# Routed experts in one fused kernel: tiles sorted by the chunk of their first row, and pick rows summed beside the last expert groups

## The chip, the cores and the metric

The kernel runs on one core of a Trainium2 chip. The metric is the device time of one execution in microseconds. Three runs of the kernel before took 598.46, 595.2 and 590.54 us, median 595.2. The profile is of one execution; its times count from the first instruction.

## The reference, cut to what matters

Everything is in 32-bit floats. A token is a row of 256 numbers; there are 4096.

```python
x = layernorm(x + attention(x))                       # 4096 tokens x 256, 16 heads
scores = sigmoid(x @ router_weight.T)                 # 32 experts in 4 groups of 8
topk_idx = the 4 best of the experts in the 2 best groups (by scores + bias)
topk_w   = 2.5 * scores[topk_idx] / sum of them
for each token and each of its 4 picks e:
    h = silu(x @ gate_w[e].T) * (x @ up_w[e].T)       # 128 wide
    mixed += topk_w * (h @ down_w[e].T)               # back to 256
shared = (silu(x @ sg.T) * (x @ su.T)) @ sd.T         # 256 wide, every token
x = layernorm(x + mixed + shared)
```

## The kernel before

**Chunks.** The tokens are cut into 8 chunks of 512 (four tiles of 128). Attention, first layernorm, router and shared expert run chunk by chunk, software-pipelined in an order written out by hand for each engine. In `route` and `place` VectorE finds each token's four experts and its rank within each expert; ranks are counted over all chunks so far by `count_picks` on TensorE, whose result ScalarE copies to `ranks_sb` (its last 32 columns are the running totals per expert, which start at 128). POOL then scatters each token's row, with its label and weight, to the expert's region in DRAM (`scatter_rows`, 128 indirect DMAs, L534). The rows of an expert therefore lie in the order of the tokens.

**The table.** When all chunks are ranked, VectorE works out which tiles of 128 rows there are (from L1677, 14 steps that wait for each other by the semaphore `b`): for each expert as many tiles as it needs, aligned to the end of its rows, the experts one after the other. TensorE transposes the result, VectorE packs it into `tab`, and the engines read tile addresses and expert numbers from it.

**The expert loop.** The tiles are worked off in groups of four, a group being two pairs. There are 34 groups in this run (136 tiles). In each pair SP loads two tiles of rows (L477), TensorE turns them over (L1292) and multiplies by gate and up weights, ScalarE copies the transposed rows (L876) and takes the tanh (L894), VectorE copies the next pair's gate and up weights from the big weight tile to a fixed place (`copy_weights`, L1754), forms the gated product (L1779, L1785) and copies labels (L1747, L1762, L1769), TensorE multiplies by the down weights one pair later, ScalarE scales and copies the result (`copy_y`, L885), and POOL scatters the result rows by label to `pick_rows` in DRAM (L568), where the four rows of a token lie together. Each engine has its own loop over the groups, written once in `quads_with_ends` with the first and the last group apart; they meet only through semaphores. Two buffers stand behind each step.

**The tail.** When the last scatter has landed, SP reads all `pick_rows` back, chunk by chunk in the order 5, 6, 7, 0, 1, 2, 3, 4 (`LAST_ORDER`), four loads of 512 KB each into four buffers (L494). VectorE adds picks 0 and 1 to 2 and 3 (`add_picks`, L1804), TensorE sums the two halves and the token's own row `sx` in PSUM through an identity matrix (`sum_rows`, L1348, L1350), with the shared expert's down product for the chunks 5 to 7 (`sum_down`). For chunks 0 to 4 `sx` holds that product already. VectorE takes mean and variance (`moments`), POOL the reciprocal root (`invert_sums`, L583), ScalarE scales (`finish`, L912) and issues the write of the output (L918). `matmul` is recorded at L933 wherever the helper `mm` issues it.

Of the kernel before, what the change touches and what calls it, by code (L numbers as in the profile page):

```python
# [13 lines left out]
P = 128  # L14
# [10 lines left out]
EPS = 1e-5  # L25
# [9 lines left out]
ZWAYS = 4  # L35
# [7 lines left out]
LAST_ORDER = (5, 6, 7, 0, 1, 2, 3, 4)  # L43
# [14 lines left out]
assert MAXTILES + QUAD <= SLOTS  # L58

# [5 lines left out]
def build(nc, xT, x, wqkv, wfc, wr, rbias, wsgu, wsd, wgu, wd, out):  # L65
# [7 lines left out]
    with ExitStack() as ctx:  # L73
# [76 lines left out]
        def x1_of(b):  # L150
# [25 lines left out]
        dstats = [sb(f"dstats{i}", [P, TPC, 6]) for i in range(2)]  # L176
        dmv = [sb(f"dmv{i}", [P, TPC, 2]) for i in range(2)]
        dveps = [sb(f"dveps{i}", [P, TPC]) for i in range(2)]
        drstd = [sb(f"drstd{i}", [P, TPC]) for i in range(2)]
        dnm = [sb(f"dnm{i}", [P, TPC]) for i in range(2)]  # L180

        cnt_u = sb("cnt_u", [P, NE], U32)
        ntile_u = sb("ntile_u", [P, NE], U32)
        ntile = sb("ntile", [P, NE])
        tend = sb("tend", [P, NE])
        ones_e = over(prod, 25 * DM - NE, NE)
        past = sb("past", [P, 2, NE])
        pend = sb("pend", [P, 2, NE])
        slot_e = sb("slot_e", [P, 2])
        slot_first = sb("slot_first", [P, 2])  # L190
        slot_base = sb("slot_base", [P, 2])
        spare = sb("spare", [P, NE + 1])
        jump = sb("jump", [P, NE])
# [21 lines left out]
        zt = [over(wgu_sb, i * TPC * TOPK * DM, TPC * TOPK, DM).rearrange("p (t k) c -> p t k c", k=TOPK)  # L215
              for i in range(ZWAYS)]
        o2 = [over(wd_sb, i * TPC * DM, TPC, DM) for i in range(2)]
# [13 lines left out]
        d_a d_ps dst_ready dmv_ready dveps_ready drstd_ready dnm_ready o2_ready stored0 stored1""".split()  # L231
# [6 lines left out]
        z_loaded = [[sem(f"z_loaded{i}_{t}") for t in range(TPC)] for i in range(ZWAYS)]  # L238
        stored = [S[f"stored{i}"] for i in range(2)]

        NSMALL = 5 * 16
        NCONST = 12
# [3 lines left out]
        block = ctx.enter_context(nc.Block())  # L246

# [5 lines left out]
        def n_quads(eng):  # L253
            eng.wait_ge(S["tab_ready"], 1)
            return eng.value_load(tab[0:1, QUADS:QUADS + 1], min_val=NTOK * TOPK // P // QUAD - 2,
                                  max_val=(MAXTILES + QUAD - 1) // QUAD - 2) + 2
# [11 lines left out]
        def _(sp):  # L268
# [216 lines left out]

            for par in range(2):
                sp.wait_ge(y_scattered[par], quads * 32)

            for g in range(CH):
                if g >= ZWAYS:  # L490
                    sp.wait_ge(S["d_ps"], TPC * (g - ZWAYS + 1))
                for t in range(TPC):
                    at = (LAST_ORDER[g] * TPC + t) * P
                    sp.dma_start(zt[g % ZWAYS][:, t, :, :],  # L494
                                 z.rearrange("(n k) c -> n k c", k=TOPK)[at:at + P, :, :])\
                        .then_inc(z_loaded[g % ZWAYS][t], 16)

        @block.gpsimd
        def _(pool):
# [24 lines left out]
            assert NCONST == 12  # L524
# [54 lines left out]
            def invert_sums(g, step, first, last):  # L579
                pool.wait_ge(S["dveps_ready"], step + 1)  # L580
                if g >= 2:
                    pool.wait_ge(S["o2_ready"], g - 1)
                pool.tensor_tensor(drstd[g % 2][:, first:last], dveps[g % 2][:, first:last], neg_half[:, first:last],  # L583
# [7 lines left out]
        def quads_with_ends(eng, quads, body):  # L591
            body(0, 0, False, True)
            body(0, 1, True, True)
            with eng.Fori(1, quads - 1) as quad:
                body(quad, 0, True, True)
                body(quad, 1, True, True)
            body(quads - 1, 0, True, True)
            body(quads - 1, 1, True, False)

        @block.scalar  # L600
        def _(act):
# [298 lines left out]

            copy_xT(0, 0)
            quads_with_ends(act, quads, pairs)
# [995 lines left out]
```

## Time and profile before

| | |
|---|---|
| runs of the kernel | 598.46, 595.2, 590.54 us, median 595.2 |
| profiled execution | span 591.0 us (its time outside the span isn't recorded) |
| PE (TensorE) | busy 557.3 us, 94% |
| DVE (VectorE) | busy 372.0 us, 63% |
| ACT (ScalarE) | busy 278.8 us, 47% |
| POOL | busy 289.8 us, 49% |
| moved by DMA | 135.34 MB, 229 GB/s over the span |
| expert loop | about 311 to 526 us |
| reads of the tail | 32 loads of 512 KB, 14.7 us from issue to landing in the median |

A busy share is time in which an engine had an instruction under way. Matmuls are pipelined, and one that waits for its predecessor counts as busy, so a TensorE at 100% isn't at its peak. "issue" as the cause of idle time means that nothing the profile shows held the engine up. A releaser is the work whose end let the waiting instruction start.

### The profile page before, as it was taken

Reading aid. Unit: us, or ns where it says so; the run is one execution under the profiler, and the core shown is the slowest. Engines: PE = TensorE matmul, PEld = TensorE weight load, DVE = VectorE, ACT = ScalarE, POOL = GpSimd, SP = SyncE. Lnnn points to the kernel's source line nnn. Section 1 sums busy time; section 2 is a strip of 40 time slices with the busy share of each in tenths; the row PEclk is TensorE's granted clock in tenths of the full one; section 3 lists DMA queues with packets and bytes.
Section 4 is the critical chain, followed back from the end, with each engine's and each line's share of the span. In section 5 each row is a group of like instructions: output and inputs, shape, how many; then the busy total and the mean of one; then the engine's idle time right before and its main releaser. Section 6 shows DMA issues by size and latency. Waiting matters only on the chain.

```text
span 591.0 us, 16304 instructions
## 1 busy us (share of the span) xinstructions
PE 557.3 (94%) x4916; PEld 437.1 (74%) x4917; DVE 372.0 (63%) x1250; ACT 278.8 (47%) x561; POOL 289.8 (49%) x301
## 2 busy tenths in 40 slices
PE   5989999999989999999969999999999999999985
PEld 2446578677665766675529999999999999887863
DVE  2032657698885887679544666666666665634774
ACT  2334453765837575253213555555555554530234
POOL 5000000654777765667741666666666665660221
PEclk9999999999999999999987999999999999999998
DMA  7999978987899799799423555555555554528996
GB/s 260 249 237 230 236 220 201 277 271 193 267 248 287 224 322 391 268 395 343 171 93 96 168 165 164 162 172 163 160 167 168 180 171 153 172 91 353 414 413 246
DMA packets 125820, 135.34 MB, mean 229 GB/s; under 512 B 76872, under 2 KB 107087, under 8 KB 125136
## 3 DMA queue, kind: packets, MB, share of 16 engines
q1 hardware_dynamic: 108288, 95.92, 54.3%
q0 software_dynamic: 12672, 34.10, 15.2%
q10 hardware_dynamic: 4816, 4.74, 2.3%
q8 instruction: 27, 0.44, 0.3%
q14 instruction: 17, 0.14, 0.1%
HBM read 74.79 MB, written 60.96 MB: 230 GB/s over the span
## 4 chain that ended last, share of the span: by engine, by line
PE 63%; DMA 15%; SPq 6%; issue 5%; POOL 4%; DVE 3%; ACT 2%; ACTq 0%; POOLq 0%; DVEq 0%
PE bank L933 54%; PE bank L1292 5%; DMA wgu_sb<-pick_rows 4%; DMA o_slots<-wgu_sb 4%; DMA wd_sb<-o_slots 3%; POOL expert_rows L534 3%; PE bank L1350 2%; DMA expert_rows<-stage,pos 2%; SPq L319 1%; SPq L328 1%; SPq L299 1%; PE bank L1348 1%; PE bank L981 1%; DMA q_slots<-wd_sb 1%; SPq L285 1%
## 5 line engine op out<-in xcount | busy, mean ns | idle before, releaser
L568 POOL DMA_INDIRECT pick_rows<-prod,ids x134 | 131.2, 979 | 93.9 <-ACT prod L885 46.2
L534 POOL DMA_INDIRECT expert_rows<-stage,pos x128 | 129.1, 1008 | 57.0 <-issue 34.8
L933 PE MATMUL bank<-prod 128*128 128x128 f32 x1088 | 135.0, 278 | 1.0 <-issue 1.0
L933 PEld LDWEIGHTS bank<-prod 128*128 128x128 f32 x1088 | 128.9, 195 | 1.7 <-issue 1.6
L933 PE MATMUL bank<-wd_sb,wqkv_sb 128*128 128x512 f32 x192 | 91.5, 614 | 6.5 <-DMA wqkv_sb<-in_wqkv 5.9
L1754 DVE COPY prod<-wgu_sb 128x512 f32 x136 | 54.1, 440 | 54.5 <-issue 51.8
L885 ACT ACTIVATE prod<-bank,kept 128x256 f32<-128x256 f32 x136 | 57.0, 470 | 37.7 <-PE bank L933 35.1
L933 PEld LDWEIGHTS bank<-wgu_sb 128*32 128x32 f32 x2048 | 58.6, 136 | 16.8 <-issue 13.6
L933 PE MATMUL bank<-wd_sb,prod 128*128 x272 | 70.1, 380 | 0.8 <-DVE prod L1785 0.8
L933 PE MATMUL bank<-wgu_sb 128*32 128x64 f32 x2048 | 65.8, 296 | 2.2 <-DMA wgu_sb<-k_slots 2.2
L933 PEld LDWEIGHTS bank<-wd_sb,wqkv_sb 128*128 128x128 f32 x192 | 35.1, 194 | 41.6 <-issue 35.8
L527 POOL TENSOR_TENSOR rstdt<-vepst,neg_half 128x4 f32<-128x4 f32 x8 | 9.0, 1129 | 100.2 <-DVE vepst L1396 100.2
L894 ACT ACTIVATE prod<-bank 128x256 f32<-128x256 f32 x68 | 26.1, 384 | 61.2 <-PE bank L933 61.2
L933 PEld LDWEIGHTS bank<-wd_sb,prod 128*128 128x128 f32 x272 | 46.5, 191 | 4.7 <-issue 1.2
L933 PE MATMUL bank<-prod,wsgu_sb 128*128 128x512 f32 x96 | 45.1, 618 | 2.8 <-DVE hsT L1461 2.8
L1292 PE MATMUL bank<-ident,prod 128*128 128x128 f32 x272 | 41.9, 278 | 3.1 <-DMA prod<-expert_rows 3.1
L876 ACT ACTIVATE prod<-bank 128x512 f32<-128x512 f32 x68 | 40.6, 597 | 4.2 <-PE bank L1292 4.2
L1292 PEld LDWEIGHTS bank<-ident,prod 128*128 128x128 f32 x272 | 34.4, 143 | 10.8 <-DMA prod<-expert_rows 4.2
L1414 DVE TENSOR_REDUCE smax<-bank 128x32 f32<-128x512 f32 x16 | 10.9, 679 | 47.2 <-PE bank L933 47.2
L618 ACT ACTIVATE stage<-sx 128x1024 f32<-128x1024 f32 x32 | 34.1, 1067 | 9.7 <-DMA expert_rows<-stage,pos 7.1
L912 ACT ACTIVATE wd_sb<-bank,dnm,drstd 128x256 f32<-128x256 f32 x32 | 15.6, 563 | 45.4 <-DVE dnm L1811 25.9
L933 PEld LDWEIGHTS bank<-prod,wsgu_sb 128*128 128x128 f32 x96 | 18.2, 196 | 24.0 <-issue 19.7
(148 smaller groups left out, 774.6 us busy)
## 6 DMA issues: line engine op xcount, KB each, us to landing
prod<-expert_rows SPq DMA_DIRECT2D x136, 132.0 KB
wgu_sb<-pick_rows SPq DMA_DIRECT2D x32, 512.0 KB, 14.7
wgu_sb<-in_wgu SPq DMA_DIRECT2D x2, 2560.0 KB, 13.4
expert_rows<-pad_rows SPq DMA_DIRECT2D x4, 1056.0 KB, 19.0
wd_sb<-in_xT SPq DMA_DIRECT2D x8, 512.0 KB, 4.8
q_slots<-wd_sb SPq DMA_DIRECT2D x16, 256.0 KB
k_slots<-wd_sb SPq DMA_DIRECT2D x16, 256.0 KB
wgu_sb<-q_slots SPq DMA_DIRECT2D x16, 256.0 KB
```

What stands on the lines that cost most here:

```text
L534: pool.indirect_dma_start(xs, bass.IndirectOffsetOnAxis(ap=pos[e % 2][:, i, k:k + 1], axis=0), stage[:, i, k, :], None, bounds_check=XROWS ...
L568: pool.indirect_dma_start(z, bass.IndirectOffsetOnAxis(ap=index[:, j:j + 1], axis=0), rows[:, j, :], None, bounds_check=TOPK * NTOK - 1, o ...
L618: act.activation(stage[:, i, :, 0:DM], x1_of(e)[:, i, :].unsqueeze(1).broadcast_to([P, TOPK, DM]), ACT.Copy)
L876: act.activation(xtT[par][:, :], banks[2][:, :], ACT.Copy).then_inc(S["cX_copied"], 1)
L885: last = act.activation(to[:, j, :], banks[6 + par][:, j * DM:(j + 1) * DM], ACT.Copy, scale=kept[par][:, j, 1:2])
L894: act.activation(cth[par][:, :], banks[par][:, 0:2 * P], ACT.Tanh, scale=0.5)\
L912: done = act.activation(o2[g % 2][:, t, :], banks[2 * (g % 4) + t // 2][:, (t % 2) * DM:(t % 2 + 1) * DM], ACT.Identity, bias=dnm[g % 2][: ...
L933: return pe.matmul(dst, lhsT, rhs, start=(k == 0), stop=(k == n - 1))
L1292: last = pe.transpose(banks[2][:, c:c + P], xt[par][:, j, k * P:(k + 1) * P], ident[:, :])
L1350: last = pe.matmul(sum_of(g, t), ident[:, :], zt[g % ZWAYS][:, t, k, :], start=False, stop=(k == 1 and (b < DOWN_AT_ONCE or t % 2 == 1)))
L1414: dve.tensor_reduce(smax[:, hf, :], score_view(hf), AX, ALU.max).then_inc(S["smax"], 1)
L1754: last = dve.tensor_copy(ws[par][:, j, :], wgu_sb[:, bass.ds(expert(word, slot + j) * (KC * 2 * EI), KC * 2 * EI)])
```

## The change

Tiles are no longer listed expert by expert. Each belongs to one of six classes: the chunk (0 to 4, or later) in which its first row lies. The table lists class by class, and by expert within a class. To this end `place` keeps the running totals of the first five chunks (`cums`), and the table is worked out for 6 x 32 = 192 virtual experts. The number of tiles is the same. After the early classes are through, all picks of the early chunks have been computed, some groups before the end; assertions bound by how much.

That is used twice. In each of the 16 groups ahead of the last, ScalarE loads one tile of 128 tokens of the chunks 0 to 3 (their 4 x 256 pick values, 512 KB) after the group's first pair, and VectorE adds them to `sx` in three additions after its second pair. And SP loads chunk 4 when four groups are left. The tail then reads the chunks 5, 6 and 7 only. The chunks 0 to 3 take their statistics directly from `sx`; outputs are written in place in `sx` and stored from there, in the order 0 to 7, and the waits on output buffers are gone.

```diff
+def groups_behind(c):
+    left = NTOK * TOPK - (c + 1) * CT * TOPK
+    return -(-(left - NE * (P - 1)) // P) // QUAD
+SUM_LAG = 3
+SUM_GROUPS = FIRST_TILES            # 16
+SUM_START = SUM_GROUPS + 1
+LATE_GROUPS = groups_behind(FIRST_CHUNKS)      # 4
...
+        early_z = wsgu_sb.rearrange("p k c -> p (k c)")
+        early_sum = wqkv_sb.rearrange("p k c -> p (k c)")[:, 2 * CT:2 * CT + 2 * DM]
...
 # SP
+            for par in range(2):
+                sp.wait_ge(y_scattered[par], quads * 32 - 32 * LATE_GROUPS)
+            load_picks(FIRST_CHUNKS)
             for par in range(2):
                 sp.wait_ge(y_scattered[par], quads * 32)
-            for g in range(CH):
-                if g >= ZWAYS:
-                    sp.wait_ge(S["d_ps"], TPC * (g - ZWAYS + 1))
...
+            for g in range(FIRST_CHUNKS + 1, CH):
+                load_picks(g)
...
-        def quads_with_ends(eng, quads, body):
+        def quads_with_ends(eng, quads, body, beside=None):
             body(0, 0, False, True)
             body(0, 1, True, True)
-            with eng.Fori(1, quads - 1) as quad:
+            with eng.Fori(1, quads - (SUM_START if beside else 1)) as quad:
                 body(quad, 0, True, True)
                 body(quad, 1, True, True)
+            if beside:
+                with eng.Fori(0, SUM_GROUPS) as tile:
+                    quad = eng.snap(eng.to_reg(quads - SUM_START + tile))
+                    body(quad, 0, True, True)
+                    beside(quad, tile, 0)
+                    body(quad, 1, True, True)
+                    beside(quad, tile, 1)
 # ScalarE
+            def load_early(quad, tile, par):
+                if par:
+                    return
+                act.wait_ge(S["e_free"], tile + 1)
+                for i in range(2):
+                    act.wait_ge(y_scattered[i], quad * 32 - 32 * SUM_LAG)
+                act.dma_start(early_z[:, :], z.rearrange("(n k) c -> n (k c)", k=TOPK)[bass.ds(tile * P, P), :])\
+                    .then_inc(S["e_z"], 16)
 # VectorE
             def place(e):
                 dve.wait_ge(S["rk"], RK * e + 1)
+                if e < CLASSES - 1:
+                    dve.tensor_copy(cums[:, e, :], ranks_sb[:, TPC, :])
...
+            at(dve.tensor_tensor(classes(behind_u[:, NE:], CLASSES - 1),
+                                 total.unsqueeze(1).broadcast_to([P, CLASSES - 1, NE]), cums[:, :, :], ALU.subtract))
...
+            at(dve.tensor_tensor(lens[:, :], whole[:, 0:VE], whole[:, NE:], ALU.subtract))
...
+            at(dve.tensor_tensor_scan(tend[:, :], ones_v[:, :], lens[:, :], 0.0, ALU.mult, ALU.add))
...
+            def sum_early(quad, tile, par):
+                if par == 0:
+                    return
+                dve.wait_ge(S["e_z"], tile * 16 + 16)
+                dve.tensor_tensor(early_sum[:, :], early_z[:, 0:2 * DM], early_z[:, 2 * DM:], ALU.add)\
+                    .then_inc(S["e_free"], 1)
+                dve.wait_ge(S["e_free"], tile + 2)
+                dve.tensor_tensor(early_sum[:, 0:DM], early_sum[:, 0:DM], early_sum[:, DM:], ALU.add)\
+                    .then_inc(S["e_half"], 1)
+                dve.wait_ge(S["e_half"], tile + 1)
+                dve.tensor_tensor(sx[:, bass.ds(tile * DM, DM)], sx[:, bass.ds(tile * DM, DM)], early_sum[:, 0:DM],
+                                  ALU.add).then_inc(S["e_sum"], 1)
...
+            dve.wait_ge(S["e_sum"], FIRST_TILES)
+            moments(0, 0, TPC)
+            moments(1, 0, TPC)
+            add_picks(4, range(TPC))
+            moments(2, 0, TPC)
+            scale_mean(0, 0, 0, TPC)
...
-BSTEPS = 14
+BSTEPS = 22
```

## Rows read from the trace of the kernel before

**Rows 1.** Windows by stage: window, length, busy us of each engine, clock, DMA share, GB/s

```profile
0.00:309.00 309.00, 289.44 (x3044) 189.94 (x3045) 197.16 (x660) 146.86 (x257) 145.51 (x156) 0.99 0.85 257
...
365.00:502.00 137.00, 137.00 (x1064) 130.06 (x1062) 88.95 (x308) 75.39 (x177) 85.50 (x89) 1.00 0.53 167
...
536.00:580.50 44.50, 41.01 (x185) 33.83 (x183) 32.22 (x95) 9.76 (x21) 8.30 (x6) 1.00 1.03 410
```

**Rows 2.** Timeline of VectorE, one group: start, length, line, operation, [idle before <-releaser]

```profile
441.88 0.77 DVE L1754 COPY prod<-wgu_sb 128x512 f32 x2 [0.79 <-issue]
...
443.39 0.16 DVE L1762 CAST ids<-kept 128x2 uint32<-128x2 f32 x1
443.69 0.35 DVE L1769 COPY kept<-meta 128x4 f32<-128x4 f32 x1
...
448.06 0.76 DVE L1754 COPY prod<-wgu_sb 128x512 f32 x2 [0.79 <-issue]
```

**Rows 3.** Timeline of all engines in the same group, ScalarE's part

```profile
442.18 0.38 ACT L894 ACTIVATE prod<-bank 128x256 f32<-128x256 f32 x1 [0.82 <-PE bank L933]
...
443.05 0.84 ACT L885 ACTIVATE prod<-bank,kept 128x256 f32<-128x256 f32 x2 [0.48 <-PE bank L933]
```

**Rows 4.** Timeline of all engines around a late scatter, 500 to 515 us

```profile
500.11 0.17 DVE L1762 CAST ids<-kept 128x2 uint32<-128x2 f32 x1 [1.03 <-DMA pick_rows<-prod,ids]
...
503.11 2.02 PE L933 MATMUL bank<-prod 128*128 128x128 f32 x16 [0.96 <-issue]
...
508.37 0.92 DVE L1754 COPY prod<-wgu_sb 128x512 f32 x2 [0.82 <-PE bank L933]
...
514.64 0.90 DVE L1754 COPY prod<-wgu_sb 128x512 f32 x2 [0.83 <-PE bank L933]
```

**Rows 5.** VectorE by line and form: busy us, mean ns of one, idle before, releaser

```profile
L1785 DVE TENSOR_TENSOR prod<-prod,bank 128x256 f32<-128x256 f32 x68 | 28.7, 421 | 5.3
...
L1804 DVE TENSOR_TENSOR wgu_sb<-wgu_sb 128x512 f32<-128x512 f32 x32 | 21.7, 690 | 22.1 <-DMA wgu_sb<-pick_rows 22.0
```

**Rows 6.** DMA issues: count, KB each, median us from issue to landing

```profile
wd_sb<-in_xT SPq DMA_DIRECT2D x8, 512.0 KB, 4.8
...
prod<-in_x SPq DMA_DIRECT2D x8, 512.0 KB, 5.6
```

**Rows 7.** Timeline of all engines in the tail

```profile
530.15 0.97 POOL L568 DMA_INDIRECT pick_rows<-prod,ids_last  x1 [0.30 <-issue]
532.61 17.64 SPq L494 DMA_DIRECT2D wgu_sb<-pick_rows  x23
...
535.90 0.69 DVE L1804 TENSOR_TENSOR wgu_sb<-wgu_sb 128x512 f32<-128x512 f32 x1 [10.02 <-DMA wgu_sb<-pick_rows]
...
553.72 1.93 ACT L912 ACTIVATE wd_sb<-bank,dnm,drstd 128x256 f32<-128x256 f32 x4 [3.06 <-DVE dnm L1811]
...
555.68 0.38 ACTq L918 DMA_DIRECT2D out<-wd_sb  x1
...
580.90 1.29 DVE L1804 TENSOR_TENSOR wgu_sb<-wgu_sb 128x512 f32<-128x512 f32 x2
```

**Rows 8.** Timeline where the table is worked out, VectorE and TensorE

```profile
281.71 0.17 DVE L1677 TENSOR_SCALAR cnt_u<-ranks_sb 128x32 uint32<-128x32 f32 x1
...
284.22 0.16 DVE L1702 TENSOR_TENSOR slot_row<-slot_base,slot_first 128x2 f32<-128x2 f32 x1
...
285.01 0.69 DVE L1461 SCALAR_TENSOR_TENSOR hsT<-hsT,bank 128x512 f32<-128x512 f32 x1
...
287.55 7.03 PE L933 MATMUL bank<-prod,wsgu_sb 128*128 128x512 f32 x16
```

**Rows 9.** Windows where TensorE stood idle, and one behind

```profile
32.90:35.10 2.20, 0.04 (x1) 0.00 (x0) 0.00 (x0) 0.60 (x1) 0.00 (x0) 1.00 1.07 281
...
296.00:298.50 2.50, 0.31 (x2) 0.00 (x1) 2.05 (x4) 1.08 (x2) 1.94 (x2) 1.00 0.30 108
...
301.00:303.50 2.50, 2.50 (x4) 0.94 (x4) 0.00 (x0) 0.00 (x0) 1.94 (x2) 0.54 0.30 108
```

More of the change, by code:

```diff
@@ L42 @@
 DOWN_AT_ONCE = 5
[L43 removed]
+SUM_BANKS = {4: 6, 5: 0, 6: 2, 7: 4}
 ROW = DM + 8
@@ L58 @@
 assert MAXTILES + QUAD <= SLOTS
+def groups_behind(c):
[4 more added lines that the diff above has]
+SUM_START = SUM_GROUPS + 1
+for _t in range(FIRST_TILES):
+    assert SUM_START - _t + SUM_LAG <= groups_behind(_t // TPC)
+LATE_GROUPS = groups_behind(FIRST_CHUNKS)
+COUNTED_FROM = SUM_START + SUM_LAG + 2
+assert LATE_GROUPS == 4 and NTOK * TOPK // P // QUAD > COUNTED_FROM
 def chunk(n):
@@ L175, in build @@
         pos = [sb(f"pos{i}", [P, TPC, TOPK], U32) for i in range(2)]
[L176 to L188, printed above, removed]
+        late = wsel.rearrange("p t k e -> p (t k e)")
+        dstats = [over(late, g * TPC * 6, TPC, 6) for g in range(CH)]
+        dmv = [over(late, 192 + g * TPC * 2, TPC, 2) for g in range(CH)]
+        dveps = [over(late, 256 + g * TPC, TPC) for g in range(CH)]
+        drstd = [over(late, 288 + g * TPC, TPC) for g in range(CH)]
+        dnm = [over(late, 320 + g * TPC, TPC) for g in range(CH)]
+        cums = sb("cums", [P, CLASSES - 1, NE])
+        region_e = sb("region_e", [P, NE])
+        behind_u = over(prod, 0, VE).bitcast(U32)
+        whole_u = over(prod, VE, VE).bitcast(U32)
+        whole = over(prod, 2 * VE, VE + NE)
+        ends = over(prod, 3 * VE + NE, NE)
+        first_row = over(prod, 3 * VE + 2 * NE, VE + NE)
+        lens = over(prod, 4 * VE + 3 * NE, VE)
+        tend = over(prod, 5 * VE + 3 * NE, VE)
+        past = over(prod, 6 * VE + 3 * NE, 2, VE)
+        pend = over(prod, 8 * VE + 3 * NE, 2, VE)
+        assert 10 * VE + 3 * NE <= 2048
+        jump = over(wfc_sb.rearrange("p k c -> p (k c)"), 0, VE)
+        ones_v = over(wfc_sb.rearrange("p k c -> p (k c)"), VE, VE)
         slot_e = sb("slot_e", [P, 2])
+        slot_u = sb("slot_u", [P, 2], U32)
+        slot_m = sb("slot_m", [P, 2], U32)
         slot_first = sb("slot_first", [P, 2])
         slot_base = sb("slot_base", [P, 2])
-        spare = sb("spare", [P, NE + 1])
-        jump = sb("jump", [P, NE])
         slot_row = sb("slot_row", [P, 4])
@@ L213, in build @@
         ws = [over(prod, 8 * DM + 4 * ROW + 8 * P + i * 2 * KC * 2 * EI, 2, KC * 2 * EI) for i in range(2)]
[L215 to L217 removed]
+        early_z = wsgu_sb.rearrange("p k c -> p (k c)")
+        early_sum = wqkv_sb.rearrange("p k c -> p (k c)")[:, 2 * CT:2 * CT + 2 * DM]
+        zt = {g: over(wgu_sb, (g - 5) * TPC * TOPK * DM, TPC * TOPK, DM).rearrange("p (t k) c -> p t k c", k=TOPK)
+              for g in range(FIRST_CHUNKS + 1, CH)}
+        zt[FIRST_CHUNKS] = over(stage.rearrange("p t k r -> p (t k r)"), 0, TPC * TOPK, DM)\
+            .rearrange("p (t k) c -> p t k c", k=TOPK)
         banks = [bank(f"bank{i}") for i in range(8)]
@@ L1687, in _ @@
+            after()
             for c in range(2):
@@ new lines, in _ @@
+            scale_mean(3, 3, 0, TPC)
+            moments(4, 0, TPC)
+            add_picks(5, (2, 3))
+            scale_mean(4, 4, 0, TPC)
+            add_picks(6, (0, 1))
+            moments(5, 0, TPC)
+            add_picks(6, (2, 3))
+            add_picks(7, (0, 1))
+            scale_mean(5, 5, 0, TPC)
+            moments(6, 0, TPC)
+            add_picks(7, (2, 3))
+            moments(7, 0, 2)
+            scale_mean(6, 6, 0, TPC)
+            moments(7, 2, TPC)
+            scale_mean(7, 7, 0, 2)
```

183 lines of the change are left out of this document (92 added, 91 removed).

## The prediction

> **What bounds the kernel now.** I read the windows by stage first, then the chain of waits, then the loop engine by engine. In the stages [rows 1] the reader is to see two limits. From 365 to 502 us, the steady part of the expert loop, TensorE is busy in all 137 us at full clock while VectorE shows only 89 us of work and the DMA engines half a share. From 536 to 580.5 us the DMA share is 1.03 at 410 GB/s: this is the tail that reads all pick rows back (16.8 MB) while it writes outputs. The chain of waits names reads of pick rows for most of it. So the tail is paid in bytes, the loop in TensorE time, and the change moves bytes from the tail into the loop.
>
> The 65% of VectorE in the loop misleads. A group (two pairs, four tiles) repeats every 6.18 us: the weight copy at 441.88 comes again at 448.06 [rows 2]. Before each weight copy stands 0.8 us of "issue", which is sequencer work (the value load and its address arithmetic) that no other engine holds up. The tanh that the next step needs [rows 3] ends at 442.56, before VectorE's own weight copies do (442.65): it waits for nobody there.
>
> The trace holds an accident that tests this [rows 4]. At 500.11 VectorE had waited 1.03 us for a scatter; TensorE then stood idle 0.96 us before 503.11. Nearly all of it passed through. Nor was it made good: from 508.37 to 514.64 a group took 6.27 us. **VectorE's own chain is as long as TensorE's.** Whatever is put into it lengthens the loop.
>
> **The change, part by part.**
>
> *Early sums, 16 groups.* After the second pair of each group VectorE waits for an early load and does three dependent additions, one of 128x512 and two of 128x256. Prices: 0.69 us for 128x512 (the pick addition of the tail) and 0.42 for 128x256 (the second gate product) [rows 5], 1.53 in all. With hops of 0.03 between dependent steps and some 0.15 of register work before the first wait, the chain from the label cast to the next kept copy becomes 0.15 + 0.72 + 0.45 + 0.05 + 0.34 = 1.71 us in place of the 0.30 between 443.39 and 443.69 [rows 2]; that 0.30 is the loop's branch, now hidden under the last addition. Added: 1.4, and I take 1.5 for the register arithmetic on the tile number. The group then takes 6.25 + 1.5 = 7.75 us against 6.18: 1.57 x 16 = **+25 us**. Lower bound: 1.2 per group (the additions' 1.53 less the 0.30 hidden), +19. Upper: 2.2 (all three start to start, with 0.6 of register work), +35. TensorE, ScalarE and POOL then wait; none of them adds to it.
>
> *The early load.* ScalarE issues it after it has copied the y rows of the previous pair. That copy needs the kept labels, which VectorE now makes only after its additions. Counted from their end: 0.4 for the kept copy, 0.84 for the two y copies [rows 3], 0.38 for the issue (as in rows 7), so about 1.6 to 1.8. VectorE needs the rows at 7.75 - 1.5 = 6.25. The load may take 4.5 us. Loads of the same 512 KB took 4.8 and 5.6 us from issue to landing [rows 6], in a stage whose DMA share is 0.85 [rows 1]; the loop has 0.53, and with the load (0.52 MB at 410 GB/s is 1.28 us of 7.75) about 0.6. The first load of the tail, with the engines free, is issued at 532.61 and its addition starts at 535.90 [rows 7], 3.3 us. Between 3.3 and 5.6 I take 4.6, a share of 0.6 lying between the two: **+1.5 us** over 16 groups for what comes late. Its end points are 0 and 16 x (1.8 + 5.6 - 6.25) = 18. On ScalarE the issue stands ahead of the next xT copy, which has over 1 us in hand.
>
> The Trainium skill ("DMA: Bandwidth & Descriptors", section "Anatomy of one DMA — SWDGE (gpsimd) path") gives about 2.0 us plus bytes at 436 GB/s for the software path; taken as an estimate here that would be 3.2 us for 512 KB, and the load would never be late. The rows show longer landings, in busier stretches.
>
> *Other work in the loop.* Counters for groups gain a few register steps on each engine; a third loop body costs a fresh start of code. Chunk 4's four loads go out on SP's queue, past the last row loads, which are issued by then, and meet the last scatters: **+1 us** together, between 0 and 3.
>
> *The tail.* The reads fall from 32 to 12 loads of 512 KB, 16.8 to 6.3 MB. SP still waits for the last scatter, whose landing sets the start at 532.6. VectorE meanwhile does the statistics of chunks 0 and 1 and adds chunk 4, but the reciprocal roots of POOL stand behind its scatters until 531.1, so the first output write goes out near 537, and then one of 512 KB each 2.3 us (1.93 for four activations, 0.38 for the issue). Until the last read lands the engines move 6.3 MB of reads and about 3.1 of writes: 9.4 MB / 410 GB/s = 23 us, plus 1.5 of ramp: near 557. In the profile the last pair of pick additions starts at 580.90 and the span ends 10.1 later; that closing chain is unchanged. 580.9 - 557 = **-23.5 us**. Bounds: no write before the last read, -29; all 4.2 MB of writes first, -20. VectorE's work for eight chunks of statistics and four of additions is some 27 us, spread from 526 on, so it isn't the limit but near it.
>
> *The table.* Tiles get 192 virtual experts where there were 32. The chain from 281.71 to 284.38 [rows 8] has 14 steps; now 22, most 192 to 384 wide. From 0.16 us for 2 elements [rows 8] and 0.69 for 512 [rows 5] an element costs 1.04 ns: some 2,430 more elements give 2.5 us, eight steps at 0.12 another 1.0: 3.5 us longer. Behind it stands the gate product (285.01) that the gate matmuls at 287.55 wait for; they start 1.7 us later, and of that some 1.5 us reaches the loop's start, through the last gate product, which stands ahead of the first weight copy on VectorE. Five more copies of 32 columns in the placement, 0.2 each, lie partly beside POOL: **+2 us** in all, between 0 and 4.5. The number of tiles stays the same, since the same whole tiles are only sorted otherwise.
>
> **The sum.** 25 + 1.5 + 1 + 2 - 23.5 = +6; I keep **+5**, as the tail's start may gain a little from less crowded last groups. The span 591.0 becomes 596. No time of the profiled execution is given beside its span; the span stands 4.2 under the median of 595.2, which I carry over: **600 us**.
>
> **Rivals.**
> 1. *The additions fall into VectorE's idle time* (faster). For it: 0.8 us of "issue" before each weight copy, two per group, looks like room for 1.5 us. Against: the sequencer itself is at work there, and rows 4 show a delay going through. If only 0.4 per group remains: 6.4 + 1 + 2 - 23.5 = -14, 581 us. It decides once the loop grows by less than 0.5 us a group. The low bounds of all terms (19 + 0 + 0 + 0 - 29) end at -10. Chance 0.15.
> 2. *The load lands late* (slower). ScalarE's issue waits for the kept labels, these for the additions, these for the load: a ring, where each microsecond of landing beyond 4.5 is paid 16 times. At 5.6 us it costs 18 in place of 1.5: +21, 616 us; at 5.2, 610. It decides from 5.0 us. With the additions at their upper bound the same sign comes out. Chance 0.25.
> 3. *TensorE's clock falls.* Its idle stretch would be 1.6 us in each group. At 296 to 298.5 us TensorE was idle 2.2 us, and the granted clock then fell to its lower level, 1.2 GHz (0.54 as a mean of 301 to 303.5); after another 2.2 us at 32.9 it stayed at 2.4 GHz [rows 9]. Part of a group at the lower level costs about 1.2 us (2.5 x 0.46), most of which the idle stretch absorbs. Only with late loads would idle stretches pass 2 us; +10 on top, 610 to 625. Chance 0.04, part of slower. The Trainium skill ("TensorE: Matmul & The Clock Gate", section "What's actually happening") says that the slow state is the default and activity releases it; by that the thinner loop is at risk. The trace has both outcomes for the same idle time.
>
> The forecast keeps 0.56. **How the numbers follow.** A change of 2% is 11.9 us, about what a measurement of this kernel can tell from no change: faster is under 583.3, slower over 607.1. Faster gets 0.16 (rival 1 and a corner of the bounds), slower 0.27 (rivals 2 and 3 with the upper bound of the additions), within 0.57. The range reaches from 586 (additions and tail near their better bounds) to 616 (rival 2 at 5.6 us), leaving a tenth outside on each side.
>
> **What would show it.** Timeline of VectorE in the last groups: weight copy to weight copy every 7.6 to 7.9 us over two pairs, the 128x512 addition waiting for the DMA under 0.3 us, TensorE idle 1.6 us before one of two gate stages. Groups before them at 6.18. Last pick addition about 24 us after the start of the tail's reads, not 48. A loop start 1 to 3 us later. I am wrong if early groups stay near 6.2 us (rival 1), or if the additions name the DMA for over a microsecond each (rival 2).

## The result, and the profile after

The changed kernel takes **604.2 us** (median of 6 runs, 601.85 to 605.41) against 596.9 us (590.54 to 599.53) for the kernel before beside it: ratio **1.0149**, 95% interval 1.0110 to 1.0187. Slower by 1.5%. The profiled run took 601.85 us around a span of 600.1 us, 9.1 us more than the 591.0 of before. Here and below the ratios are over fast runs alone and the medians over all runs, so the two don't agree to the last digit.

Windows by stage of the changed kernel (length, busy us of PE, PEld, DVE, ACT, POOL, then clock, DMA share, GB/s). They answer to [rows 1]; the loop now has two stages, in the first two rows; the third is the tail.

```profile
330.00:420.00 90.00, 90.00 (x702) 85.53 (x700) 58.62 (x204) 49.74 (x117) 56.81 (x59) 1.00 0.53 163
443.00:553.00 110.00, 86.81 (x632) 76.31 (x631) 68.61 (x224) 47.21 (x106) 50.98 (x53) 1.00 0.60 191
569.50:589.50 20.00, 20.00 (x94) 17.61 (x93) 13.02 (x45) 10.82 (x23) 4.90 (x5) 1.00 0.98 376
```

Up to 420 us the loop is the old one. From 443 to 553 us, in the early groups, TensorE works in 79% of the time. The tail's window is 20 us where it was 44.5, and the DMA engines are full in it as before.

VectorE's timeline through one early group, which answers to [rows 2] (start, length, line, operation, idle before):

```profile
463.68 0.76 DVE L1820 COPY prod<-wgu_sb 128x512 f32 x2 [1.14 <-issue]
...
465.57 0.17 DVE L1813 COPY meta<-prod 128x4 f32<-128x4 f32 x1
466.81 0.80 DVE L1820 COPY prod<-wgu_sb 128x512 f32 x2 [1.07 <-PE bank L983]
...
468.31 0.33 DVE L1828 CAST ids<-kept 128x2 uint32<-128x2 f32 x1
468.38 0.69 DVE L1862 TENSOR_TENSOR wqkv_sb<-wsgu_sb 128x512 f32<-128x512 f32 x1
469.10 0.42 DVE L1865 TENSOR_TENSOR wqkv_sb<-wqkv_sb 128x256 f32<-128x256 f32 x1
469.69 0.42 DVE L1868 TENSOR_TENSOR sx<-sx,wqkv_sb 128x256 f32 x1 [0.16 <-DVE wqkv_sb L1865]
470.50 0.17 DVE L1835 COPY kept<-meta 128x4 f32<-128x4 f32 x1 [0.38 <-issue]
470.77 0.17 DVE L1813 COPY meta<-prod 128x4 f32<-128x4 f32 x1
472.11 0.76 DVE L1820 COPY prod<-wgu_sb 128x512 f32 x2 [1.17 <-issue]
```

A "meta copy" here is the copy of a pair's labels and weights out of the loaded rows, a "kept copy" the second copy of them, by which the results are scaled and scattered, a "cast" the one that makes row numbers of the labels. Three readings. The group takes 472.11 - 463.68 = **8.43 us** against 6.18. The first addition starts 0.07 us after the label cast: it waits for no read. From cast to kept copy it is 2.19 us in place of 0.30, and from each meta copy to its weight copy 1.24 and 1.34 us, where the plain loop has about 1.0, as in this half of a group before:

```profile
444.14 0.17 DVE L1747 COPY meta<-prod 128x4 f32<-128x4 f32 x1
445.13 0.82 DVE L1754 COPY prod<-wgu_sb 128x512 f32 x2 [0.82 <-issue]
```

TensorE in the same group, and at the first early groups, where the granted clock fell once (a gate stage of 16 matmuls took 3.55 us and not 2.02):

```profile
429.80 3.55 PE L983 MATMUL bank<-prod 128*128 128x128 f32 x16 [2.79 <-ACT prod L919]
...
464.55 2.02 PE L983 MATMUL bank<-prod 128*128 128x128 f32 x16 [1.70 <-ACT prod L919]
```

The tail, answering to [rows 7] (the second row is the last pair of pick additions):

```profile
569.10 6.19 SPq L523 DMA_DIRECT2D wgu_sb<-pick_rows  x12
...
590.02 1.40 DVE L1884 TENSOR_TENSOR wgu_sb<-wgu_sb 128x512 f32<-128x512 f32 x2
```

From the start of the reads to that pair it is 20.9 us, against 580.90 - 532.61 = 48.3.

**The account.** Cut both spans at the start of the loop's third gate stage (318.01 us after, 319.71 before) and at the end of the last down matmul (561.83, 526.54). Ahead of the loop -1.7, loop +37.0, tail 38.3 against 64.5 = -26.2: together +9.1. The tail gave what was asked of it, and the loop cost more than that. The -1.7 is noise: the first gate stage happened to run at the lower clock before (3.62 us) and at full clock after (2.02), and in the 14 profiles of this case the second group's first weight copy starts anywhere from 316.4 to 323.2 us, over code that hardly differs up to there.

### The profile page after: what moved, and what is told of

The parts are those of the page before. It is cut to its first block, busy times and chain, and to the rows that moved or that the text cites. A ratio compares the mean times of both kernels' runs of the same rounds, so it can differ in the third digit from the quotient of the medians.

```text
span 600.1 us, 16345 instructions
## 1 busy us (share of the span) xinstructions
PE 543.7 (91%) x4820; PEld 419.1 (70%) x4821; DVE 383.9 (64%) x1294; ACT 281.9 (47%) x561; POOL 287.1 (48%) x302
## 4 chain that ended last, share of the span: by engine, by line
PE 59%; DMA 11%; DVE 10%; issue 7%; DVEq 4%; ACT 3%; SPq 3%; POOL 2%; ACTq 1%; POOLq 0%
PE bank L983 54%; PE bank L1342 3%; DMA wgu_sb<-pick_rows 2%; DVEq L293 2%; DMA prod<-expert_rows 2%; DMA expert_rows<-stage,pos 2%; DVE prod L1820 1%; DVE prod L1845 1%; PE bank L1031 1%; DMA pick_rows<-prod,ids 1%; DVE wqkv_sb L1862 1%; DVE wqkv_sb L1865 1%; DVE ids L1828 1%; DMA o_slots<-wgu_sb 1%; DMA wd_sb<-o_slots 1%
## 5 line engine op out<-in xcount | busy, mean ns | idle before, releaser
L572 POOL DMA_INDIRECT expert_rows<-stage,pos x128 | 127.8, 999 | 59.2 <-issue 33.8
L983 PE MATMUL bank<-wd_sb,wqkv_sb 128*128 128x512 f32 x192 | 92.8, 621 | 6.7 <-DMA wqkv_sb<-in_wqkv 6.0
L983 PE MATMUL bank<-wd_sb,prod 128*128 x272 | 70.1, 380 | 1.2 <-DVE prod L1851 1.2
L1342 PEld LDWEIGHTS bank<-ident,prod 128*128 128x128 f32 x272 | 32.6, 141 | 17.1 <-issue 9.5
L983 PEld LDWEIGHTS bank<-prod,wsgu_sb 128*128 128x128 f32 x96 | 18.2, 196 | 23.9 <-issue 19.7
L670 ACT ACTIVATE wd_sb<-bank 128x512 f32<-128x512 f32 x32 | 19.4, 608 | 27.8 <-PE bank L983 25.3
```

The costliest lines, as they stand in the source:

```text
L572: pool.indirect_dma_start(xs, bass.IndirectOffsetOnAxis(ap=pos[e % 2][:, i, k:k + 1], axis=0), stage[:, i, k, :], None, bounds_check=XROWS ...
L670: act.activation((QT, KT)[j // 2][:, j % 2, :], banks[j % 2][:, :], ACT.Copy)\
L983: return pe.matmul(dst, lhsT, rhs, start=(k == 0), stop=(k == n - 1))
L1342: last = pe.transpose(banks[2][:, c:c + P], xt[par][:, j, k * P:(k + 1) * P], ident[:, :])
```

## The experiments

All ratios are to the kernel before, in the runs beside them. The means are over the 15 whole groups, weight copy to weight copy, that hold early additions; "loop" is from the second group's first weight copy to the last weight copy of all, "rest" from there to the end of the span.

| Kernel | median us | ratio (95%) | group, mean us | loop | rest |
|---|---|---|---|---|---|
| before | 596.9 | 1 | 6.30 | 202.9 | 70.1 |
| after | 604.2 | 1.0149 (1.0110 to 1.0187) | 8.58 | 239.3 | 44.4 |
| additions one column wide | 596.4 | 1.0011 (0.9971 to 1.0052) | 7.89 | 228.0 | 44.7 |
| no early reads | 602.7 | 1.0130 (1.0069 to 1.0191) | 8.41 | 236.6 | 44.5 |
| early groups written out | 602.2 | 1.0167 (1.0088 to 1.0246) | 8.23 | 233.3 | 44.2 |
| before, sorted table | 596.5 | 1.0012 (0.9972 to 1.0051) | | | |
| second loop, no additions | 605.5 | 1.0123 (1.0064 to 1.0183) | 6.84 | 211.6 | 70.6 |
| additions on GpSimd | 667.2 | 1.1215 (1.1156 to 1.1275) | 11.92 | 293.4 | 49.8 |
| chunk 4 read in the tail | 616.1 | 1.0322 (1.0271 to 1.0372) | 8.57 | 239.0 | 52.8 |
| chunk 0 read one a group | 595.6 | 0.9997 (0.9962 to 1.0032) | 6.58 | 206.7 | 66.8 |
| chunk 0 read at the end | 596.1 | 0.9976 (0.9927 to 1.0024) | 6.30 | 206.9 | 67.9 |
| base outside the loop | 600.3 | 1.0072 (1.0031 to 1.0113) | 8.26 | 235.8 | 44.4 |
| base outside, written out | 599.1 | 1.0074 (1.0035 to 1.0113) | 8.13 | 233.9 | 45.0 |
| the same, no early reads | 585.3 | 0.9830 (0.9781 to 0.9879) | 7.22 | 217.9 | 46.8 |

For each the same 15 groups are meant, also where they hold no additions. The profiled run of the sorted table took 601.3 us, 4.8 above that kernel's median, so its loop isn't compared. The kernels with narrow additions or without early reads leave out part of the result, the sums of chunks 0 to 3.

### What the additions' width costs

```
-    dve.tensor_tensor(early_sum[:, :], early_z[:, 0:2 * DM], early_z[:, 2 * DM:], ALU.add)
+    dve.tensor_tensor(early_sum[:, 0:1], early_z[:, 0:1], early_z[:, 2 * DM:2 * DM + 1], ALU.add)
```

The two additions behind it are cut to one column in the same way, so the sums of chunks 0 to 3 are left out.

> The three additions of each early group keep their place, their waits and their registers, but are one column wide instead of 512, 256 and 256, so the sums of chunks 0 to 3 are left out. Theory A (VectorE's own chain sets the group): the widths are worth about 0.5 + 0.25 + 0.25 = 1.0 us of the 8.42 us of a group, so a group takes 7.4 us, and the time falls by 16 us against the changed kernel, to about 588. The 1.2 us that then still lie above 6.18 are waits between dependent steps and register work. Theory B (the early load, through ScalarE's queue, sets the group): a group stays at 8.2 to 8.4, time 601 to 604.

Measured: 596.4 us, no different from the kernel before, and groups of 7.72 us at best. VectorE's timeline in that kernel:

```profile
498.89 0.32 DVE L1828 CAST ids<-kept 128x2 uint32<-128x2 f32 x1
498.96 0.25 DVE L1862 TENSOR_TENSOR wqkv_sb<-wsgu_sb 128x1 f32<-128x1 f32 x1
499.27 0.16 DVE L1865 TENSOR_TENSOR wqkv_sb<-wqkv_sb 128x1 f32<-128x1 f32 x1
499.59 0.16 DVE L1868 TENSOR_TENSOR sx<-sx,wqkv_sb 128x1 f32 x1 [0.16 <-DVE wqkv_sb L1865]
500.39 0.17 DVE L1835 COPY kept<-meta 128x4 f32<-128x4 f32 x1 [0.64 <-issue]
```

With next to no elements, cast to kept copy still takes 1.50 us. The elements are 0.69 us of the 2.24 added a group; the other 1.55 are there without them, and the runs below take them apart. I had put 1.0 us to the elements and 1.2 to the rest, and so expected 588. Theory B falls: a group doesn't stay at 8.2 to 8.4.

### Whether the read is what VectorE waits for

```
-    act.dma_start(early_z[:, :], z.rearrange("(n k) c -> n (k c)", k=TOPK)[bass.ds(tile * P, P), :])...
-    dve.wait_ge(S["e_z"], tile * 16 + 16)
```

The additions then add what lies in the buffer; the sums of chunks 0 to 3 are left out.

> The 16 early loads and VectorE's wait for them are left out; the three additions run over what lies there, so the sums of chunks 0 to 3 are left out. Theory A: VectorE waits only some 0.1 us for the load, so a group stays within 0.2 us of 8.42 and the time falls by 1 to 4 us (the first groups, where the load was late, and the DMA queues), to 600 to 603. Theory B: a group falls to 7.7 us or less and the time by 11 us or more, to 593 or less.

Measured: 602.7 us, steady groups of 8.37 to 8.45, such as this one (8.40 us):

```profile
476.42 0.76 DVE L1818 COPY prod<-wgu_sb 128x512 f32 x2 [1.18 <-issue]
...
484.82 0.76 DVE L1818 COPY prod<-wgu_sb 128x512 f32 x2 [1.15 <-issue]
```

**Rival 2 falls**: without reads the steady group is as long. Only the first two early groups differ, 8.45 and 8.43 against 9.62 and 9.50: in the changed kernel one scatter comes late there, TensorE stands idle 2.79 us, and the lower clock follows (the row at 429.80 above).

### What constants in place of computed values give

```
-    with eng.Fori(0, SUM_GROUPS) as tile:
+    for tile in range(SUM_GROUPS):
```

> The loop over the 16 early groups is written out, on VectorE and ScalarE, so that the tile number is a constant: no branch, no arithmetic on the tile number in waits and addresses. The computation is the same. Theory A1 (of the 2.24 us that a group grew, 0.6 lie before the weight copies and 0.4 before the kept copy, and both come from the tile number and the branch): a group falls by 0.5 to 1.0 us, the time by 8 to 16, to 588 to 596. Theory A2 (the extra gaps come from the group number being a computed register, which it still is): a group falls by 0.1 to 0.4 us, time 598 to 603. Against both: 16 groups of code that is fetched once may cost waits of a microsecond each, time 605 or more.

Measured: 602.2 us, groups of 7.8 to 8.9, mean 8.23. VectorE's timeline:

```profile
498.30 0.33 DVE L1828 CAST ids<-kept 128x2 uint32<-128x2 f32 x1
...
499.89 0.17 DVE L1835 COPY kept<-meta 128x4 f32<-128x4 f32 x1
500.16 0.17 DVE L1813 COPY meta<-prod 128x4 f32<-128x4 f32 x1
501.45 0.88 DVE L1820 COPY prod<-wgu_sb 128x512 f32 x2 [1.12 <-issue]
```

Cast to kept copy is now 1.59 us: 0.60 less than in the changed kernel, so that much was the loop's branch and the register work on the tile number. The gap ahead of the weight copy stays at 1.29: it has another source. The mean group fell by 0.35 us and the time, which its four runs (597 to 608) don't tell from the changed kernel's, lies in the range of Theory A2; both causes are at work.

### The table alone

The kernel before with the sorted table of 192 virtual experts (the table's part of the diff alone), its tail and loop as they were.

> The kernel before with the sorted table alone (six classes, 192 virtual experts, 22 steps), its loop and its tail as before. If the table costs what I predicted, 599; if the loop's start is not delayed, as in the profile of the changed kernel, within 1 us of the kernel before, about 597. A time under 594 would mean that the order of the tiles itself helps, one over 600 that it costs in the loop.

Measured: ratio 1.0012. The table's chain is longer, 5.85 us in the changed kernel (280.70 to the next instruction at 286.55) against 2.59 (281.71 to 284.30), but nothing of it can be measured at the end; the interval allows -1.7 to +3.0 us. In the changed kernel's profile the chain happened to start 1.0 us sooner and TensorE stood idle 0.81 us for it; it turned the result over from 287.08, against 287.12 before.

### The group number alone

```
-    with eng.Fori(1, quads - 1) as quad:
+    with eng.Fori(1, quads - 17) as quad:
+        body(quad, 0, True, True)
+        body(quad, 1, True, True)
+    with eng.Fori(0, 16) as tile:
+        quad = eng.snap(eng.to_reg(quads - 17 + tile))
```

> The kernel before with the sorted table, its tail of eight chunks, and its last 16 groups run by a second loop whose group number is worked out from the loop's variable, as in the changed kernel, on TensorE, ScalarE and VectorE; no additions, no early reads. Theory A (the unpredicted 0.3 us in each half of a group is register work that the worked-out group number brings): those 16 groups take 6.7 to 6.8 us, and the time is 605 to 607 us against 596 us. Rival (it belongs to the additions or to the reads they need): the groups stay at 6.18 us and the time is 595 to 598 us.

Measured: 605.5 us, groups of 6.73 to 6.80 but for one of 8.20. Theory A holds. A loop that computes nothing more than the old one costs 9 us, 8.7 in the traces (211.6 against 202.9). The kernel has the sorted table too, which by itself changed nothing that can be measured. One group of it, and the gap in its second half:

```profile
472.94 0.76 DVE L1786 COPY prod<-wgu_sb 128x512 f32 x2 [1.15 <-PE bank L948]
...
478.35 0.17 DVE L1779 COPY meta<-prod 128x4 f32<-128x4 f32 x1
479.66 0.76 DVE L1786 COPY prod<-wgu_sb 128x512 f32 x2 [1.14 <-PE bank L948]
```

From meta copy to weight copy it is 1.25 and 1.31 us in the two halves here, as in the changed kernel, and 0.98 (median) in the first loop of either. In the compiled order VectorE has three register instructions ahead of the load of the group's word, where the plain loop has one; that count is from the compiled program, since the profile doesn't record such instructions. Two more of them in each half lengthen the group by 0.56 us, 0.28 a half. (The trace puts the gap down to TensorE, whose gate matmuls had ended 0.5 us before.)

### Base outside the loop, and both together

```
+    start = eng.snap(quads - SUM_START)
     with eng.Fori(0, SUM_GROUPS) as tile:
-        quad = eng.snap(eng.to_reg(quads - SUM_START + tile))
+        quad = start + tile
```

The compiled order has one register instruction again. The second kernel also writes the groups out, as above.

> The changed kernel with one edit: the first early group's number is put into a register ahead of the loop, so that in the loop VectorE works the group's address out with one register instruction instead of three, in each half of a group. Theory A (the two added instructions in each half cost the 0.56 us a group that the second loop without additions showed): early groups fall from 8.42 to 7.86 us, 16 of them give back 9 us, and the time is 595 us. Rival (what the address costs lies behind the additions anyway, or another engine's part of the group bounds it then): groups of 8.3 us or more, and 602 to 604 us.

> The same, with the 16 early groups written out one after the other, so that the additions' addresses and the values that they wait for are constants. Theory A (register work is what separates the 8.42 us of the changed kernel from additions alone): the written-out groups took 7.92 us with the three instructions, less 0.56 us gives 7.36 us; 16 groups give back 17 us of the changed kernel's, the tail keeps its 26 us, and the time is 586 to 589 us, 1 to 2% below the kernel before. Rival (the groups then come to another bound, late scatters or TensorE): 7.9 us, and 595 us or more.

Measured: 600.3 and 599.1 us. With the base outside the loop the gap is back at 0.97 us in one half of each group and at 1.0 to 1.2 in the other, so the register work had made it:

```profile
482.30 0.17 DVE L1814 COPY meta<-prod 128x4 f32<-128x4 f32 x1
483.26 0.76 DVE L1821 COPY prod<-wgu_sb 128x512 f32 x2 [0.79 <-PE bank L984]
```

Both are a little better than the changed kernel, but with means of 8.26 and 8.13 us where 7.86 and 7.36 were expected; the first has groups of 7.9 to 9.2, the second single groups of 7.3 among others of 8.5. So VectorE's chain was no longer the only bound. The written-out kernel shows the next one:

```profile
504.38 0.17 DVE L1829 CAST ids<-kept 128x2 uint32<-128x2 f32 x1 [0.42 <-DMA pick_rows<-prod,ids]
504.39 0.84 ACT L929 ACTIVATE prod<-bank,kept 128x256 f32<-128x256 f32 x2 [1.83 <-DMA pick_rows<-prod,ids]
505.10 0.69 DVE L1863 TENSOR_TENSOR wqkv_sb<-wsgu_sb 128x512 f32<-128x512 f32 x1 [0.55 <-DMA wsgu_sb<-pick_rows]
```

Late scatters hold the label cast and ScalarE's y copies, and the read itself holds the addition.

### Without the reads, once more

The written-out kernel with the base outside, less the reads and VectorE's wait for them; the sums of chunks 0 to 3 are left out.

> The 16 early groups written out with the first group's number in a register, as before, and without the reads of chunks 0 to 3 and VectorE's wait for them: the additions add what lies in the buffer, so the sums of these chunks are left out. In the run with the reads the groups took 7.3 us at best and 8.1 us in the mean, with VectorE, ScalarE and TensorE waiting for late scatters, for the read itself or for a group's rows. Theory A (the 512 KB read of each group makes those transfers late, and is the next bound once VectorE's part is shorter): without the reads all groups take 7.3 to 7.4 us, the loop is 12 us shorter than with them, and the time is 585 to 589 us. Rival (the written-out groups are uneven for another reason, their code or the pairing of the halves): groups stay at 7.9 to 8.1 us in the mean and the time is 596 to 599 us.

Measured: **585.3 us**, groups of 7.05 to 7.59, mean 7.22, such as this one (7.18):

```profile
479.43 0.92 DVE L1819 COPY prod<-wgu_sb 128x512 f32 x2 [0.61 <-issue]
...
486.61 0.94 DVE L1819 COPY prod<-wgu_sb 128x512 f32 x2 [0.60 <-issue]
```

Theory A holds. Waits by engine over 443 to 545 us of the kernel with reads (total, times, longest):

```profile
ACT prod L929 <- DMA pick_rows<-prod,ids: 19.2, 11, 2.9
...
DVE ids L1829 <- DMA pick_rows<-prod,ids: 5.0, 6, 2.1
...
PE bank L1343 <- DMA prod<-expert_rows: 3.3, 5, 0.9
```

and over 443 to 531 us of the kernel without (in the same stretch ScalarE's wait in the kernel with reads is 16.9 us, 10 times):

```profile
ACT prod L929 <- DMA pick_rows<-prod,ids: 1.6, 2, 0.9
```

The windows of 443 to 531 us, first with the reads, then without:

```profile
443.00:531.00 88.00, 73.63 (x512) 65.10 (x511) 59.30 (x186) 36.18 (x86) 44.36 (x44) 0.96 0.64 199
```

```profile
443.00:531.00 88.00, 77.96 (x581) 71.18 (x580) 65.09 (x207) 42.36 (x99) 49.53 (x49) 1.00 0.49 148
```

So the reads cost the steady groups nothing while VectorE's chain takes 8.42 us, and 0.9 us a group (8.13 - 7.22) once it takes 7.2. The edit also takes away ScalarE's issue of each read, 0.35 us a group; that this isn't the cause follows from the waits, and from the reads of chunk 0 further down, which SyncE issues and which cost as much. The Trainium skill ("DMA: Bandwidth & Descriptors", section "Queues, rings and completion order") says that each engine takes turns between the queues it has work for, a packet at a time. Late scatters and row loads beside a large read agree with that; no run here separates it from plain lack of bandwidth.

### The additions on GpSimd

The three additions leave VectorE's loop and stand on GpSimd behind the group's four scatters.

> The changed kernel with its early additions issued on GpSimd, behind the group's four scatters, instead of on VectorE. Theory A (the loop pays because VectorE has no idle time, and GpSimd had 2.9 us of it in each early group): if the three additions take GpSimd less than that, the early groups fall from 8.42 to 6.2 to 6.8 us, the tail keeps its 26 us, and the time is 574 to 582 us. Rival (GpSimd's additions are several times slower than VectorE's 1.5 us, or hold VectorE up): its scatters come late, the groups take 8.4 us or more, and the time is 604 us or more.

Measured: 667.2 us, groups of 11.1 to 12.8. The time is the rival's, but not by its first reason. GpSimd, ScalarE and TensorE in one of them:

```profile
516.82 1.30 POOL L614 TENSOR_TENSOR wqkv_sb<-wsgu_sb 128x512 f32<-128x512 f32 x1
518.19 0.72 POOL L617 TENSOR_TENSOR wqkv_sb<-wqkv_sb 128x256 f32<-128x256 f32 x1
518.41 0.35 ACTq L967 DMA_DIRECT2D wsgu_sb<-pick_rows  x1
518.93 0.60 ACT L936 ACTIVATE prod<-bank 128x512 f32<-128x512 f32 x1 [5.23 <-DMA pick_rows<-prod,ids]
519.11 0.72 POOL L620 TENSOR_TENSOR sx<-sx,wqkv_sb 128x256 f32 x1 [0.20 <-POOL wqkv_sb L617]
519.58 1.12 PE L1359 MATMUL bank<-ident,prod 128*128 128x128 f32 x4 [3.75 <-ACT prod L936]
...
520.49 3.62 PE L1000 MATMUL bank<-prod 128*128 128x128 f32 x16
```

The additions themselves take 2.7 us, 1.8 times VectorE's. The damage is a ring, work that waits for itself one turn back. ScalarE's next read goes out 0.3 us after GpSimd's first addition ends (518.12), since it waits for the buffer that this frees; the addition stands behind scatters, and the scatters behind ScalarE's copies of the y rows. ScalarE stands 5.2 us, TensorE 3.75, and TensorE's clock is 0.80 in the mean from 450 to 600 us. The trace names a scatter for ScalarE's wait; that it is the buffer is my reading of the times. Whether GpSimd could do the additions with a second buffer wasn't tried.

### Where reads of chunk 4 or chunk 0 are cheap

The changed kernel with chunk 4's four reads put behind the last scatter:

```
-    for par in range(2):
-        sp.wait_ge(y_scattered[par], quads * 32 - 32 * LATE_GROUPS)
-    load_picks(FIRST_CHUNKS)
     for par in range(2):
         sp.wait_ge(y_scattered[par], quads * 32)
+    load_picks(FIRST_CHUNKS)
```

> The changed kernel with one edit: the four reads of chunk 4 are issued after the last scatter instead of when four groups are left. Theory A (those reads pay in the tail what they cost in the loop): the late scatter of 6.36 us and ScalarE's wait of 3.71 us go, the loop is 2 to 4 us shorter, the tail reads 2.1 MB more and is some 5 us longer, and the time is 604 to 607 us, 1 to 3 us above the changed kernel. Rival (the late scatter comes from elsewhere): the loop keeps its length and the time is 609 us.

Measured: 616.1 us, 12 above the changed kernel, outside both. In the traces the loop is 0.4 us shorter and the rest **8.4 us longer**; the other 7 us of the spans' difference lie ahead of the loop, in the noise named above. Of the 12 us between the medians the traces explain these 8; the rest stays open. The boundary of the table, the last weight copy, hides a part of what chunk 4's reads cost the changed kernel. Behind it ScalarE waits there for a scatter, and the longest such wait without these reads is 0.8 us:

```profile
558.35 0.84 ACT L928 ACTIVATE prod<-bank,kept 128x256 f32<-128x256 f32 x2 [3.71 <-DMA pick_rows<-prod,ids]
```

From the second group's first weight copy to the start of the tail's reads it is 252.7 us with the reads in the loop and 250.7 without. So they cost 2.0 us, as Theory A said, and its error is the tail: from the start of its reads to the end it is 10.0 us longer (41.0 against 31.0), not 5. VectorE has chunk 4's additions in its order ahead of the statistics of chunks 2 and 3, and the additions must wait:

```profile
573.97 1.77 SPq L523 DMA_DIRECT2D stage<-pick_rows  x4
...
577.72 0.69 DVE L1882 TENSOR_TENSOR stage<-stage 128x512 f32<-128x512 f32 x1 [7.39 <-DMA stage<-pick_rows]
```

Then the same idea in the plain loop: the sorted table, no early additions, and chunk 0's four reads issued early into the staging buffer, one a group in one kernel and all at once, four groups from the end, in the other.

```
+    for t in range(EARLY_FROM):
+        quad = sp.snap(sp.to_reg(quads - EARLY_FROM + t))
+        load_rows(quad, 0, False)
+        load_rows(quad, 1, False)
+        if t < TPC:
+            ...
+            load_picks(0, t)
```

> The sorted table, and no additions in the expert loop: SyncE issues the four 512 KB reads of chunk 0, one a group in the last eight groups, into the staging buffer, and the tail reads seven chunks in place of eight. Theory A (in the loop VectorE pays for additions, while reads alone, issued on SyncE and landing in a buffer that nobody needs, are free): groups stay at 6.18 us, the tail loses the 2.1 MB of one chunk, some 5 us at the tail's 410 GB/s, and the time is 590 to 592 us. Rival (the reads collide with the loop's scatters and row loads, as the reads of chunk 4 did at the end of the loop of the changed kernel): each read delays a scatter by up to 4 us, the loop grows by 4 to 16 us, and the time is 596 to 606 us.

> As the run with chunk 0's reads one a group, but all four are issued at once when four groups are left. There each read made one scatter late and its group 0.95 us longer, 3.9 us in all, as much as the tail won. Theory A (a burst meets one scatter, not four): the loop grows by 1 to 2 us, the tail loses 4 to 5 us, and the time is 592 to 594 us. Rival (the burst costs as much as its parts, or the tail starts later): 596 us or more.

Measured: 0.9997 and 0.9976, no change. Read one a group, each read lengthens its group from 6.18 to 7.1 or 7.2; read at once, one scatter comes 4 us late (first row: one a group; second: at once):

```profile
491.66 0.17 DVE L1808 CAST ids<-kept 128x2 uint32<-128x2 f32 x1 [1.01 <-DMA pick_rows<-prod,ids]
```

```profile
523.05 0.17 DVE L1804 CAST ids<-kept 128x2 uint32<-128x2 f32 x1 [4.01 <-DMA pick_rows<-prod,ids]
```

Either way four reads cost the plain loop 4 us (206.7 and 206.9 against 202.9) and save 2.2 to 3.3 behind it. Both Theories A fall: a read was free only beside a VectorE chain that leaves the scatters slack. No version tried that computes the whole result beats the kernel before.

## Why the prediction came out as it did

Time and range held (600, 586 to 616; measured 604.2) and the likeliest case did. The mechanism, VectorE's chain lengthened by the additions, is shown. That the time came within 4 us is in part luck, since errors of either sign met in it. Of the signs that the prediction named, TensorE's idle of 1.6 us (1.70) and additions that don't wait for the DMA came; groups of 7.6 to 7.9 us (8.42), a tail of 24 us (20.9) and a later start of the loop did not. The terms:

- **Early additions, +25: too small.** They measure 2.24 x 16 = **+36 us**, just over the upper bound of 35. I had 1.71 us from cast to kept copy; it is 2.19, and the written-out kernel shows that I had worked out its 1.59 and left out most of the loop's register work. The second part was no term at all: the group number as a computed value, 0.28 us in each half, shown alone by the second loop (6.74 against 6.18). The two come to 1.89 + 0.56 = 2.45; some 0.2 is given back, most of it between kept copy and next meta copy (0.45 before, 0.27 after), for a reason that the trace doesn't name. By measured parts: 0.69 for elements, 0.56 for the group number, the rest issue, waits and the branch.
- **Late read, +1.5: right in the sum, wrong in the mechanism.** Steady groups don't wait for it (0.07 us after the cast). The first two cost 1.2 and 1.1 us more, by a late scatter and by one fall of the clock. The landing that I took, 4.6 us, can't be read in the changed kernel; with the additions on GpSimd the same reads took 3.7 (median).
- **Other work in the loop, +1: near nothing.** Chunk 4's reads cost 2.0 us, but only 0.4 of it ahead of the last weight copy. The late scatter of [rows 4], 1.5 us, is gone from the long groups; the profiles with short groups at the end have it (a group of 7.6 to 8.2).
- **Tail, -23.5: nearly right.** -26.2, inside -29 to -20. The start of its reads came later by 1.2 us (7.3 after the last down matmul, 6.1 before), which is the price of chunk 4's reads: without them it is 6.1 again. From there to the last additions 27.4 were saved: 20.9 us where I had 24.4. At the 368 GB/s of these 20.9 us the engines moved 7.7 MB, so by this estimate 1.4 MB of writes got in ahead of the last read and not 3.1. My working has slips: 580.9 - 557 is 23.9, and by my own rate and ramp the bounds are -31 and -21.
- **Table and front, +2: not there.** The chain grew by 3.3 us (I had 3.5), and nothing of it reached the end.
- Sum: -1.7 + 37.0 - 26.2 = +9.1 where the terms gave +6, of which I kept +5. The loop came out 9.5 above its 27.5 (25 + 1.5 + 1), the tail 2.7 and the front 3.7 below theirs, and these cancelled two thirds of it.

**Rival 1** (idle time) falls: hardly anything put into VectorE's chain was absorbed, not even two register instructions. **Rival 2** falls for this kernel, yet its cause is real. It was mostly late scatters and not the read's own landing, and it appears when the groups get shorter. **Rival 3** came once (+1.1 us); in 110 us with idle stretches of up to 1.7 us in each group the clock stayed at 2.4 GHz (1.00), and with stretches near 4 us it was 0.80. In the written-out kernel with reads and the base outside one stretch of 1.96 us was enough: the clock is 0.50 from 510.2 to 513 us, and 0.96 over the 88 us.

```profile
508.73 2.87 PE L984 MATMUL bank<-prod 128*128 128x128 f32 x16 [1.96 <-ACT prod L920]
```

**The point from which it pays.** The tail saves 26.2 us and 16 groups pay for it, so a group may grow by 1.6 us. It grows by 2.24. With nearly all register work gone and no reads, so without a full result, it grows by 7.22 - 6.18 = 1.04, and the kernel is 1.7% faster than before; with the reads in, by 8.13 - 6.18 = 1.95, and it is 0.7% slower. So the register work hid a second bound, and mending it gave only a third of what its own price promised (5 us of 17).

## What to carry to other kernels

When work goes into a chain that sets a loop's period, count every instruction of its engine, those on registers too, and compare the compiled order: a loop variable replaced by an expression cost 9 us over 16 groups. Work out the base of such an expression ahead of the loop. Before moving reads from a bandwidth-bound tail into a loop, ask which small transfers in the loop lie on its ring; these pay for each large read, here about 1 us per 512 KB, against 1.3 us that the tail saved for each of the 20 reads that left it, and 0.6 to 0.8 us for chunk 0's reads beside the plain loop.

## What the runs showed of the hardware

- Two more register instructions in VectorE's program, by the compiled order, lengthened its chain by 0.28 us, 0.14 each, nearly as long as a copy of 4 columns (0.17).
- An addition of one column took 0.16 to 0.25 us, and three dependent ones 0.8 from first start to last end; 128x512 took 0.69 on VectorE and 1.28 on GpSimd, 128x256 took 0.42 and 0.72.
- Four reads of 512 KB issued together made a scatter on another queue 4 us late, as much as four issued apart did in all.
- TensorE's clock stayed up through idle stretches of 1.7 us in every group, and fell after one of 2.79 us and, in another kernel, after one of 1.96 us.
